# Graph attention and mixture FFN on one core: the output projection of a tile pair cut into 64-row products in two PSUM banks, its two divisions placed around a copy, one normalisation an expert later

## What is computed

```python
q, k, v = (xn @ W).reshape(N, 2, 64)                  # xn: layernorm of x
scores = where(adj > 0, q * SCALE @ k.T, NEG_INF)     # [2, 4096, 4096]
sat = (softmax(scores) @ v).reshape(N, 128)           # both heads side by side
out = concat([sat[:2048] @ weightr, sat[2048:] @ weightd]) + bias
x = x + leaky_relu(out)                               # end of attention
xn = layernorm(x)
mask = one_hot(top_k(xn @ Wg + bg, 2)).sum()
x = x + sum_e mask[:, e] * (gelu(xn @ W1[e] + b1[e]) @ W2[e] + b2[e])
```

## Time and profile before

| | us |
|---|---|
| median of 3 runs | 811.79 |
| lowest and highest | 811.76, 815.22 |
| the profiled execution: its time | 814.05 |
| its span | 812.4 |
| busy: PE, ACT, DVE, POOL | 788.7, 684.4, 646.3, 474.4 |
| TensorE's mean granted clock, share of full speed | 0.997 |

### The profile page before, as it was taken

One profiled execution on the slowest core, in us unless ns is written; L12 is line 12 of the kernel. 1 busy time (PEld: TensorE's weight loads), 2 busy tenths in 40 slices (PEclk: granted clock), 3 DMA queues, 4 the chain that ended last, 5 costly groups with the idle time before them and its releaser, 6 DMA issues.

```text
span 812.4 us, 33326 instructions
## 1 busy us (share of the span) xinstructions
PE 788.7 (97%) x12576; PEld 587.7 (72%) x12576; DVE 646.3 (80%) x1470; ACT 684.4 (84%) x1099; POOL 474.4 (58%) x491
## 2 busy tenths in 40 slices
PE   4999999999999999999999999999999899999997
PEld 2467777777777777777777777777777667777775
DVE  6888998888889888888989888888974667545554
ACT  4688898888888888888888888888888799999996
POOL 4066374747556384746647474755633567676664
PEclk9999999999999999999999999999999999999999
DMA  9635344333443443334334433344200000000000
GB/s 227 117 60 87 61 71 78 66 59 61 68 72 60 64 82 58 58 58 78 64 58 72 74 61 58 61 68 72 32 1 3 1 15 15 15 13 13 13 13 14
DMA packets 40910, 45.10 MB, mean 56 GB/s; under 512 B 22168, under 2 KB 32160, under 8 KB 40864
## 3 DMA queue, kind: packets, MB, share of 16 engines
q0 software_dynamic: 9216, 33.56, 26.0%
q1 hardware_dynamic: 31216, 10.71, 5.8%
q10 hardware_dynamic: 432, 0.20, 0.1%
HBM read 71.72 MB, written 2.10 MB: 91 GB/s over the span
## 4 chain that ended last, share of the span: by engine, by line
PE 93%; DVE 2%; ACT 2%; POOL 2%; issue 1%; DMA 1%; DVEq 0%; POOLq 0%
PE ps L1106 22%; PE ps L1054 20%; PE ps L1075 18%; PE ps L1100 6%; PE ps L1233 4%; PE ps L1235 3%; PE ps L1234 3%; PE ps L1174 3%; PE ps L1175 3%; PE ps L1176 3%; PE ps L1117 2%; PE ps L1004 1%; PE ps L1012 1%; PE ps L1125 1%; PE ps L995 1%
## 5 line engine op out<-in xcount | busy, mean ns | idle before, releaser
L719 DVE CUSTOM_DVE_ANT_0 prob<-ps,mask 128x1024 f32<-128x1024 f32 x256 | 311.6, 1221 | 31.6 <-PE ps L1054 27.6
L518 ACT ACTIVATE prob<-prob,nmax 128x1024 f32<-128x1024 f32 x256 | 292.9, 1144 | 0.0
L1075 PEld LDWEIGHTS ps<-ident,prob 64*128 64x128 f32 x4096 | 152.5, 138 | 60.9 <-issue 58.2
L1106 PE MATMUL ps<-pt,v_sb 128*64 128x128 f32 x3072 | 188.9, 276 | 0.0
L1054 PE MATMUL ps<-k_half,q_row 64*128 64x512 f16 x1536 | 187.6, 376 | 0.9 <-DVE k_half L669 0.8
L1075 PE MATMUL ps<-ident,prob 64*128 64x64 f32 x4096 | 180.2, 227 | 3.1 <-ACT prob L518 1.5
L1106 PEld LDWEIGHTS ps<-pt,v_sb 128*64 128x64 f32 x3072 | 165.8, 137 | 6.8 <-issue 0.4
L445 POOL TENSOR_TENSOR prob<-prob 128x512 f16<-128x512 f32 x104 | 123.7, 1194 | 65.1 <-ACT prob L596 62.2
L343 POOL TENSOR_TENSOR pt_lo<-pt_raw,pt_hi 128x1024 f16<-128x1024 f32 x62 | 134.2, 2165 | 5.2
L538 ACT ACTIVATE pt<-ps 128x1024 f32<-128x1024 f32 x96 | 98.3, 1024 | 43.1 <-PE ps L1075 42.8
L340 POOL TENSOR_SCALAR pt_hi<-pt_raw 128x1024 f16<-128x1024 f32 x62 | 77.5, 1250 | 85.3 <-ACT pt_raw L538 70.6
(11 more groups left out here) (124 smaller groups left out, 1083.5 us busy)
## 6 DMA issues: line engine op xcount, KB each, us to landing
mask<-in_adj POOLq DMA_DIRECT2D x64, 512.0 KB, 5.6
q_row<-q_nat SPq DMA_DIRECT2D x128, 32.0 KB, 4.8
x_sb<-in_x SPq DMA_DIRECT2D x4, 512.0 KB, 6.9
out<-x_sb SPq DMA_DIRECT2D x8, 256.0 KB, 2.3
x2t_hi<-in_L_ffn_W SPq DMA_DIRECT2D x1, 1024.0 KB, 6.4
wq_sb<-in_L_gnn_Wq ACTq DMA_DIRECT2D x1, 64.0 KB, 2.7
wk_sb<-in_L_gnn_Wk ACTq DMA_DIRECT2D x1, 64.0 KB, 4.3
wv_sb<-in_L_gnn_Wv ACTq DMA_DIRECT2D x1, 64.0 KB, 5.6
```

The costliest lines, as they stand in the source:

```text
L518: act.activation(prob[:, h, cols], prob[:, h, cols], ACT.Exp, bias=nmax[:, h:h + 1], scale=-1.0, accum_out=sums[:, j, h, p:p + 1]).then_in ...
L719: dve.tensor_tensor_reduce(out=prob[:, h, col_of(p)], in0=ps[:, 2 * (u % 2):2 * (u % 2) + 2, :].rearrange("p b c -> p (b c)"), in1=mask[:, ...
L1075: ins = pe.transpose(ps[:, bank + half, t * DH:(t + 1) * DH], prob[part, h, (p * KT + t) * P:(p * KT + t + 1) * P], ident[part, part])
L1106: ins = pe.matmul(ps[dims, AV, 0:P], v_sb[:, tile, dims], probs, start=(tile == 0), stop=(tile == NT - 1))
```

## The change

Five edits. The projection's matrix is taken head by head: rows of head h of `sat_st` and of `wrd`, 64 each, give that head's 128 columns, and the two heads write to two banks, POST and AV (columns 128 to 383, beside the attention's own). In TensorE's step this stands at k = 2 between the turn of unit 4 and the scores of units 4 and 5; a wait on `post_chain` now stands before the `attend` that next writes AV. On DVE the division that adds the bias takes head 1 and stands directly after `finish_tile`, ahead of the copy of unit 4; the other takes head 0 and stays at u = 5. `keep_logits` moves from u = 4 to u = 3, ahead of `finish_tile`. The loop of TensorE becomes two loops, one for each half of the tiles, so that the choice of weight is fixed in each. In the FFN the last pair's `normalise` moves from after `combine` of expert 0 to after that of expert 1.

```diff
+        def o_part(banks, t, h):
+            first = h * P + t * D
+            return ps[:, banks[h], first:first + D]
...
-            def divide(t0, bank=POST):
+            def divide_second(t0, banks=(POST, AV)):
                 link = linker(post_chain, POST_STEPS // PAIR * t0 + 2)
                 dve.wait_ge(o_psum, t0 + PAIR)
                 for t in range(PAIR):
-                    ins = dve.scalar_tensor_tensor(o_half[:, t, :], ps[:, bank, t * HEADS * D:t * HEADS * D + D],
-                                                   rinv[:, t, 0:1], bias_b[:, :], ALU.mult, ALU.add)
+                    ins = dve.scalar_tensor_tensor(o_half[:, t, :], o_part(banks, t, 1), rinv[:, t, 1:2], bias_b[:, :],
+                                                   ALU.mult, ALU.add)
                 link(ins)
+            def divide_first(t0, banks=(POST, AV)):
+                link = linker(post_chain, POST_STEPS // PAIR * t0 + 3)
                 for t in range(PAIR):
...
+                    ins = dve.scalar_tensor_tensor(o_pre[:, t, :], o_part(banks, t, 0), rinv[:, t, 0:1], o_half[:, t, :],
+                                                   ALU.mult, ALU.add)
                 link(ins)
...
                     if finish and u == 4:
                         finish_tile(i - 2, par)
+                    if post and par == 1 and u == 4:
+                        divide_second(i - 3)
                     if prior and u in DVE_COPIES:
                         copy_pt(i - 1, u, early, last)
...
-                        if u == 4 and ready:
+                        if u == 3 and ready:
                             keep_logits(i - 5)
                         if u == 5:
-                            divide(i - 3)
+                            divide_first(i - 3)
...
-                    if early and e == 0:
+                    if early and e == 1:
                         normalise(NT - PAIR)
...
-            def out_project(t0, bank=POST):
+            def out_project(t0, m, banks=(POST, AV)):
                 pe.wait_ge(sat_ready, t0 + PAIR)
                 if not isinstance(t0, int) or t0 > 0:
                     pe.wait_ge(logit_ready, t0)
+                pe.nop(nofuse=True)
                 for t in range(PAIR):
-                    ins = pe.matmul(ps[:, bank, t * HEADS * D:(t + 1) * HEADS * D], sat_st[:, t, :],
-                                    wrd[:, t0 // (NT // 2), :, :].rearrange("p h d -> p (h d)"), start=True, stop=True)
+                    for h in range(HEADS):
+                        dims = slice(h * DH, (h + 1) * DH)
+                        ins = pe.matmul(o_part(banks, t, h), sat_st[dims, t, :], wrd[dims, m, h, :], start=True, stop=True)
                 ins.then_inc(o_psum, PAIR)
...
                         transposes(i - 1, 2 * k, early, not now)
+                    if post and par == 1 and k == AV_BLOCK:
+                        out_project(i - 3, m)
                     if now:
                         scores(i, par, 2 * k)
...
+                    if post and par == 1 and k == AV_BLOCK:
+                        pe.wait_ge(post_chain, POST_STEPS // PAIR * (i - 3) + 3)
                     if k >= AV_BLOCK and prior:
                         attend(i - 1, k - AV_BLOCK, early, whole=not now)
...
-                    if post and par == 1 and k == 2:
-                        out_project(i - 3)
...
-            pairs(pe, 6, NT, step)
+            pairs(pe, 6, NT // 2 + PAIR, step)
+            pairs(pe, NT // 2 + PAIR, NT, lambda i, par: step(i, par, m=1))
```

More of the change, by code:

```diff
@@ L761, in divide @@
                 for t in range(PAIR):
-                    ins = dve.scalar_tensor_tensor(o_half[:, t, :], ps[:, bank, t * HEADS * D:t * HEADS * D + D],
-                                                   rinv[:, t, 0:1], bias_b[:, :], ALU.mult, ALU.add)
+                    ins = dve.scalar_tensor_tensor(o_half[:, t, :], o_part(banks, t, 1), rinv[:, t, 1:2], bias_b[:, :],
+                                                   ALU.mult, ALU.add)
                 link(ins)
+            def divide_first(t0, banks=(POST, AV)):
+                link = linker(post_chain, POST_STEPS // PAIR * t0 + 3)
                 for t in range(PAIR):
-                    second = t * HEADS * D + D
-                    ins = dve.scalar_tensor_tensor(o_pre[:, t, :], ps[:, bank, second:second + D], rinv[:, t, 1:2],
-                                                   o_half[:, t, :], ALU.mult, ALU.add)
+                    ins = dve.scalar_tensor_tensor(o_pre[:, t, :], o_part(banks, t, 0), rinv[:, t, 0:1], o_half[:, t, :],
+                                                   ALU.mult, ALU.add)
                 link(ins)
@@ L904, in _ @@
             invert_sums(NT - PAIR)
-            divide(NT - PAIR, bank=PREP0 + 1)
+            divide_second(NT - PAIR, banks=(PREP0 + 1, PREP0))
+            divide_first(NT - PAIR, banks=(PREP0 + 1, PREP0))
             leaky(NT - PAIR)
@@ L1137, in logits, with step @@
                 ins.then_inc(logit_psum, PAIR)
-            def step(i, par, prior=True, now=True, drain=True, post=True, ready=True, early=False):
+            def step(i, par, prior=True, now=True, drain=True, post=True, ready=True, early=False, m=0):
                 for k in range(NU // 2):
@@ L1265, in ffn @@
                     if early and e == 1:
-                        out_project(NT - PAIR, bank=PREP0 + 1)
+                        out_project(NT - PAIR, 1, banks=(PREP0 + 1, PREP0))
                     if early and e == 5:
```

## The result

The change made the kernel very slightly slower: a median of 814.27 us (14 runs, 813.32 to 815.36) against 812.54 for the kernel before (14 runs, 811.39 to 815.22), a ratio of 1.0020 with a 95% interval of 1.0012 to 1.0029. Forecast were 810.5 us and a gain of 1.3; it lost 1.7. The sign of the small number was wrong, the range held. The profiled execution took 814.21 us, its span 812.5.

What follows compares the result with a forecast made beforehand. The prediction took TensorE's chain to bound the attention stage. From the median 811.79 us it added 1.5 for the loop through DVE and subtracted 2.8 for the FFN, giving 810.5, with an 8-in-10 range of 804.5 to 816.8.

Steps and rivals of the forecast that it cites:

- The sign of the small number: Whole kernel: slightly faster, 810.5 us against 811.79; chances 0.19 faster and 0.20 slower by over 0.5%, 0.61 within.
- The saving: Projection on TensorE: eight overlapping records take 0.44 us instead of 1.06, 0.62 less per pair, 9.3 us over 15 pairs.
- The loop through DVE: Attention step: unit 5's turn waits for copy, division and products in a chain, taking back most of the gain; chance 0.62.
- +0.1 us per pair, 1.5 us in 15 pairs: Attention step: net loss after the saved products, next turn at 204.4 instead of 204.29.
- the worst case of 0.43: Attention step: with 0.2 us at each end of the handovers, +0.43 us per pair, +6.4 us.
- The second loop: TensorE's loop in two halves adds one loop entry, costed at nothing.
- The FFN: Chunk 0: 2.15 us standstill at `down` of expert 2 goes; 2.05 us gained, 3.75 with the clock, 2.8 for the median.
- the doubt: FFN: doubted that the median execution has the half-clock stretch, which cost 1.7 us in the profiled one.
- Heads that do not overlap: Projection on TensorE: the two heads' products end 0.44 us later, 6.6 us more, 817.1 us; chance 0.12.
- A loop that does not bind: Attention: DVE reaches unit 4's copy before TensorE finishes the scores, all 0.62 us stay, 799.7 us; chance 0.06.
- FFN without gain: FFN: L930 or `x2_transpose` blocked by POOL as long as before, 813.3 us; chance 0.10.
- Something else late: Attention: something such as unit 5's mask or ACT's copy goes late by 0.3 us per pair, 815 us; chance 0.10.

Runs made afterwards that it cites:

- experiment 5: Changed kernel with the copy of unit 4 ahead of the first division on DVE and the projection between the scores of units 4 and 5: 805.20 us.
- experiment 9: Like experiment 5, but DVE's own waits on `post_chain` moved from directly behind each division to the next instruction that reads its result: 800.03 us.
- experiment 7: Like experiment 3, but the projection in its old form, two products of 128 rows and 256 columns into the one bank POST: 813.09 us.
- experiment 3: Changed kernel with only DVE's order at u = 4 turned round, the copy of unit 4 ahead of the first division: 805.72 us.
- experiment 8: Changed kernel with both divisions, not one, ahead of the copy of unit 4 on DVE: 822.80 us.
- experiment 2: Changed kernel with `normalise` of the last pair back at expert 0, so all edits but the FFN's: 817.03 us, against 812.49 for the kernel before.
- experiment 4: Kernel before with only TensorE's loop cut in two, the weight's choice left as it was: 812.14 us, ratio 0.9988.
- experiment 1: Kernel before with only the last pair's `normalise` moved from expert 0 to expert 1: 810.64 us against 812.49.
- experiment 6: Changed kernel, division still ahead of the copy of unit 4, with the projection between the scores of units 4 and 5: 818.10 us.
- experiment 10: Like experiment 3, projection still ahead of both scores, with DVE's waits on `post_chain` moved to the reader as in experiment 9: 806.79 us.

## Why the prediction was wrong, point by point

**The saving: right.** The two heads' products overlap: eight records take 0.44 us where TensorE comes to them without a wait (experiment 5). With every wait away, the turns stand 4.77 us apart (experiment 9), 0.62 less than the 5.39 of before, the 0.62 forecast. From one odd step to the next experiment 9 saves more, 36.10 - 35.39 = 0.71 us. In the new place the form alone is worth 7.4 us, 0.5 per pair (experiment 7). The Trainium skill (TensorEngine Tiling (Array Packing), Key Properties) has a drain at each change of tiling mode; the prediction refused to count it a second time, on top of the 1.06 us, and the 0.62 bears that out.

**The loop through DVE: right as a mechanism.** Taking the first division out of it gives 8.55 us back (experiment 3), putting the second in costs 8.5 more (experiment 8). About 1 of the 8.55 us is the stop, which experiment 3 lacks; in experiment 8 it is 0.55 us shorter, which hides as much of the cost.

**The failed step is the size of that term**, "+0.1 us per pair, 1.5 us in 15 pairs". Measured, it is 0.23 per pair, 3.5 us, inside the worst case of 0.43 but more than twice the value taken. In the time of the earlier trace rows the chain was:

| | forecast | measured, less 1.07 |
|---|---|---|
| `sat_st` written | 199.50 | 199.59 |
| products start | 199.60 | 199.73 |
| division starts | 200.27 | 200.49 |
| copy of unit 4 | 201.04 to 201.73 | 201.22 to 201.91 |
| turn of unit 5 | 201.8 | 202.05 |
| next turn | 204.4 | 204.59 |

No link was badly off. `sat_st` was 0.09 late, since `keep_logits` held DVE for 0.19 us (200.18 to 200.37), not 0.09; its signal to TensorE took 0.14 instead of 0.10; the products lasted 0.71 up to their last end instead of 0.63; the copy's signal took 0.14 instead of 0.07. Two links were quicker, the chained wait by 0.04 and the stretch from the turn of unit 5 to the next by 0.06. The sum, 0.19, was decisive because the term was a small difference between a saving of 0.62 and a cost of the same size. Both handovers from DVE to TensorE took 0.14 us, longer than either row that I had for them (0.06 and 0.10), and the time of the new products was put together from rows of other products.

**What the prediction lacked.** A second step failed by being absent. All edits but the last cost 4.5 us (experiment 2): 15 x 0.23 = 3.5, and the stop of 1.09 us at 98.6, which nothing in the profile of before announced. That is 3.0 more than the 1.5 forecast, and this is the whole error of the sum.

**The second loop: right** as far as can be told, nothing outside the noise (experiment 4).

**The FFN: right in its total.** Forecast were 3.75 us for the profiled execution and about 2.8 for the median. In the two profiles the time from the attention's last scores to the same product of chunk 0 fell from 642.07 - 601.84 = 40.23 to 642.24 - 605.79 = 36.45 us, by 3.78. By medians the edit gives 2.8 in the changed kernel (experiment 2) and 1.85 in the kernel before (experiment 1); the intervals of these do not separate the two. Inside the total two small items were misplaced: `x2_transpose` does not wait at all, and `gate_transpose` waits 0.41 us, not less than its 0.29 of before (DVE's `leaky` ahead of it took 1.36 us there and 1.15 before). The half clock behind the standstill came in the profiled execution of before and not in those of experiments 2 and 4, which stood still as long. Of the 51 executions of the kernel before in the three series, 12 had a mean granted clock of 0.997 or 0.998 and took 814.3 to 815.3 us; the other 39 took 810.7 to 813.2. So about one execution in four seems to have the half clock and the median one does not: the doubt was justified.

**The rivals.** Heads that do not overlap: refuted. A loop that does not bind, 799.7 us: that is not the change. Experiment 9 comes to 800.03, but by a way which that rival did not have, with three more edits; that the totals agree this well is in part luck. FFN without gain: refuted. Something else late: not in the step; the stop of 1.1 us is of that kind, a fourth of the 4.5 assumed for that rival.

**Open.** The cause of the stop "issue". It appears in the changed kernel (1.09 us) and in experiments 2 (1.36), 6 (0.88) and 8 (0.54), always at the same record of the same `attend`, near 98.6 to 99.4 us; not in the kernel before, nor in the seven other experiments. The four are just the kernels in which a division stands ahead of the copy. The traces show one thing more. Instructions come over a queue of their own in packets of 16 KB (0.59 MB in 36). Three of the eight kernels without the stop and the four with it have these packets in this stretch:

| | packets start at | TensorE goes on at |
|---|---|---|
| the kernel before | 88.35, 94.00, 99.90 | no stop |
| experiment 3 | 88.35, 94.75, 99.35 | no stop |
| experiment 5 | 87.45, 94.80, 98.35 | no stop |
| the change | 87.55, 97.40, 101.10 | 99.72 |
| experiment 2 | 88.10, 98.50, 102.15 | 100.75 |
| experiment 6 | 86.90, 97.15, 101.00 | 99.60 |
| experiment 8 | 87.35, 97.55, 101.15 | 99.77 |

Where TensorE stops, the second packet starts 9.9 to 10.4 us after the first, in all eight others 5.5 to 7.4, and TensorE goes on 2.2 to 2.5 us after that start. So it looks as if TensorE had run out of loaded instructions. Which engine the packet is for, and why it comes late only with the division first, is not shown. The number of packets is not the cause: 36 in place of 31 in every kernel with two loops, experiment 3 among them.

## What to carry to other kernels

When work on a second engine is put behind a wait for the engine that bounds the kernel, list what stands behind it there and who waits for that: here a product made 0.54 us shorter lost 0.23 us per pair because one copy had to wait for its result, and merely swapping copy and division was worth 8.55 us. Where a saving and a new loop are about equal, the handovers decide: two of them took 0.14 us where no row had shown more than 0.10. So price each at the longest row at least, and give the sign no more confidence than their sum allows. A wait written right behind the instruction that signals it holds up everything after it; put at the reader, it gave up to 5.2 us once DVE was what TensorE waited for (experiment 9), and lost 1 to 2 us where it was not (experiment 10).

## What the runs showed of the hardware that was not expected

- The same eight records took 0.44 us up to the next scores when TensorE came from other products, and 0.52 when it came from a wait (experiments 5 and 3).
- A standstill of 2.4 us on TensorE was followed by a loss of 1.7 us of clock in one profiled execution and by none in two others; over the kernel before's 51 executions the lower mean clock came in 12.
- TensorE can stop for 0.5 to 1.4 us inside a run of like products with no semaphore involved, in some kernels and not in close relatives of them. In all four kernels with the stop a packet of instructions starts 9.9 to 10.4 us after the one before it, in the eight others 5.5 to 7.4.
